# Attention and grouped feed-forward on one core: maximum pass with the norm folded in, group scalars spread by DMA, other places for the steps

## The chip, the cores and the metric

One Trainium2 chip, one core. The metric is device time in microseconds. The kernel before takes 446.42 us (median of 3 runs, 442.9 to 447.45).

## What is computed

x is (4, 256, 256): four sequences of 256 tokens with 256 channels. Two blocks are added to it in turn. In both, a two-way decayed scan (`wkv`) of a side input gives a gated input r, and the main part works on r. Cut to what matters:

```python
def qknorm(t, scale):
    return t * rsqrt(mean(t * t, -1) + 1e-6) * scale
# block 1: attention, 16 query heads on 4 key heads, head size 128, causal
q = qknorm((r @ Wq.T) by heads, q_scale); k = qknorm((r @ Wk.T) by heads, k_scale)
attn = softmax(where(causal, q @ k.T * 128 ** -0.5, min))
x = x + (attn @ v).reshape(b, t, 2048) @ Wo.T
# block 2: 64 experts in 8 groups, the best 8 of a token are kept
scores = softmax(r2 @ gate_w.T); w_e = scores kept only where in the top 8
flat = w_e[:, inv_map]              # (tokens, 8 groups, 8)
scalar = flat.sum(-1)               # one number for token and group
soft = softmax(where(flat == 0, -1e9, flat))
xg = r2 + soft @ mask_up_w          # (tokens, 8 groups, 256)
a = silu(xg @ gate_proj_w) * (xg @ up_proj_w)   # 176 rows for each group
x = x + sum over groups of scalar * (a @ down_proj_w)
```

## The kernel before

All activations lie transposed, channels on partitions. The weights of the matmuls that count are split into a high part (fp32r, ScalarE casts it) and a low part (GpSimd subtracts), and each product is three matmuls (`three`, L1103). Tokens go in two pairs of sequences (p = 0, 1) of 512 tokens.

Each engine runs a list of steps that `make_plan` (L115) writes once from a fixed order per engine (`ORDERS`, `FFN_ORDERS`), a starting list (`START`) and places for background steps (`bg`) and key and value steps (`kv`). An instruction waits only for semaphores; the order within an engine is that of its list.

- Start: the first `wkv` calls on VectorE and ScalarE, the key projections K1 and K3, and table steps R, which make a table of the experts' up projection (EX).
- Attention: 32 items m (a pair, a key head g, a sequence and a half t of it) run through a software pipeline of iterations i. An entry (kind, back) of an order treats item i - back in iteration i. A: projection of queries; ScalarE copies and squares; VectorE sums the squares (L902); N: norm of two items, ScalarE log and exp, VectorE one Newton step (`refine`, L908) to the inverse norms RQ. B: transposes of queries. C: scores on TensorE (L1176); then on VectorE (L1037) one pass per head that adds the mask to the scores, writes them to PR and gives the row maximum MX, and a small instruction (L1042) that makes the bias NBI = -MX * RQ. X: exp on ScalarE (L742, by way of L600) with scale RQ and bias NBI, which sums the row too. S: reciprocal on VectorE, multiplication on GpSimd (L587). D: transposes of the weights. E: product with V, copied to OH on ScalarE; L: OL on VectorE (L1063). F: projection with Wo. A unit u is 512 score columns: an even item has one unit of four heads with 128 keys, an odd one two units of two heads with 256 keys, 48 units in all.
- Feed-forward: 22 tiles f, 11 to a pair, of 128 of the 8 x 176 rows. GA and GB make gate and up in the banks sc and tr. GS (L1289) is one matmul of an indicator table IND with the split scalars SCX into the bank ov, and so spreads each row's group scalar over the partitions. GT: tanh on ScalarE. GU: three operations on VectorE (L1078, L1082, L1087), the third of which multiplies by ov. GH and GL split the result into OH and OL. Y(f) is TensorE's projection with the down weights, run two tiles later. Routing (`route`, L917, steps 0 to 8) makes the softmax, the top 8 and the scalars: for pair 0 in iterations 30 to 37, for pair 1 between the tiles. Step 8 transposes STS, in which the group sums stand twice, and VectorE makes the low part in rows 32 to 63 of SCX.
- The queue of SP issues every DMA, in order. Loads of weights go through three stage buffers in the order of TensorE's list (`load`, L472); each waits until the buffer's last user is done.

Of the kernel before, what the change touches and what calls it, by code (L numbers as in the profile page):

```python
# [26 lines left out]
NSTAGE, NSLOT, NPS = 3, 6, 4  # L27
# [5 lines left out]
def table_col(g):  # L33
# [24 lines left out]
    "PE": ["GA", "GB", "GS", "Y", "last", "split"],  # L58
# [18 lines left out]
def kv_k(p, half):  # L77
# [37 lines left out]
def make_plan(engine, order, ffn_order):  # L115
# [18 lines left out]
    for k, i in enumerate([25, 29]):  # L134
# [14 lines left out]
    for p, places in ((0, [3, 5, 6, 6]), (1, [20, 20, 23, 23])):  # L149
# [3 lines left out]
    for f, places in enumerate(([36, 37, 38], [45, 45, 45])):  # L153
        for kind, i in zip(("GA", "GB", "GS"), places):
# [38 lines left out]
    for st, f in zip(last, [0, 1, 2, 3, 4, 5, 6, 7, 8, 9, 10]):  # L193
# [25 lines left out]
BLOCKS = [s for s in PLAN if s[0] in ("small", "split", "ind") or s[0] == "R" and s[1] >= 6]  # L219
# [1141 lines left out]
```

## Time and profile before

| | us |
|---|---|
| median of 3 runs | 446.42 |
| lowest, highest | 442.9, 447.45 |
| the profiled execution, whole | 446.21 |
| its span, first to last instruction | 444.2 |

The span is what the profile accounts for; the other 2.0 us lie around it. Busy time is the time in which an engine has an instruction under way; overlapping instructions count once. "Idle before" is what passed on the engine before an instruction, with the one that released it. The stages follow one another: start up to about 44 us, attention up to about 331 us, then the feed-forward tiles.

### The profile page before, as it was taken

To read this page: it belongs to the slowest core of one execution; us is meant where nothing else is said; L and a number is where in the kernel's file an instruction comes from. 1 tells how busy PE (TensorE), PEld (TensorE's weight loads), DVE (VectorE), ACT (ScalarE), POOL (GpSimd) and SP (SyncE) were. 2 spreads that over 40 slices of the span, in tenths; PEclk is the share of its full clock that TensorE was granted. 3 is DMA by queue.
4 is the path that set the end of the run, shared out by engine and by line. 5 is a ranking of instruction groups with operands and counts; after the bars stand their busy time and mean duration, and the time that the engine had idled before them with its cause. 6 is when DMAs were issued, how large, how long until landed. Compare 5 with 4: busy or idle time off the path is not lost.

```text
span 444.2 us, 6572 instructions
## 1 busy us (share of the span) xinstructions
PE 380.3 (86%) x1974; PEld 305.6 (69%) x1974; DVE 336.3 (76%) x834; ACT 290.4 (65%) x675; POOL 214.8 (48%) x236
## 2 busy tenths in 40 slices
PE   0097866799998869997889798899899999999996
PEld 0086644587877557875758686777678887888884
DVE  6999577999998997577999979866657758553443
ACT  5444868699889768886789995979366334444321
POOL 4671520637553735513159121237138865687632
PEclk9998999999999997999999899999999999999999
DMA  7813410102111110110102200012112321233101
GB/s 201 312 32 106 137 43 0 49 1 97 47 49 48 49 47 0 49 49 0 47 2 82 80 0 2 0 38 71 38 53 90 106 53 56 72 108 94 61 0 47
DMA packets 11073, 26.84 MB, mean 60 GB/s; under 512 B 1312, under 2 KB 3872, under 8 KB 11040
## 3 DMA queue, kind: packets, MB, share of 16 engines
q1 hardware_dynamic: 11040, 26.44, 18.6%
q8 instruction: 16, 0.26, 0.2%
q14 instruction: 17, 0.14, 0.1%
HBM read 25.39 MB, written 1.05 MB: 60 GB/s over the span
## 4 chain that ended last, share of the span: by engine, by line
PE 49%; DVE 30%; ACT 12%; issue 6%; POOL 1%; DMA 1%; POOLq 0%; SPq 0%; DVEq 0%; ACTq 0%
PE acc L1105 4%; PE ov L1198 4%; PE acc L1106 4%; PE acc L1107 4%; PE tr L1127 4%; PE sc L1176 3%; DVE B L845 3%; DVE PR L1037 3%; DVE F L845 3%; ACT PR L600 3%; PE proj L1105 3%; PE proj L1107 2%; PE proj L1106 2%; DVE SS L902 2%; PE tr L1105 2%
## 5 line engine op out<-in xcount | busy, mean ns | idle before, releaser
L567 POOL TENSOR_TENSOR WL<-stage,WH 128x256 fp32r<-128x256 f32 x146 | 119.8, 851 | 112.7 <-ACT WH L637 112.6
L587 POOL TENSOR_TENSOR PR<-PR,RI 128x512 f32<-128x512 f32 x48 | 54.0, 1140 | 89.1 <-DVE RI L1051 89.1
L1105 PE MATMUL proj<-WH,RH 128*128 128x512 f32 x96 | 43.5, 453 | 39.3 <-DVE RL L896 22.9
L600 ACT ACTIVATE PR<-PR,NBI,RQ 128x128 f32<-128x128 f32 (+1 forms) x128 | 68.5, 546 | 1.9 <-DVE NBI L1042 1.7
L1105 PE MATMUL acc<-OH,WH 128*128 128x256 f32 (+1 forms) x172 | 55.4, 322 | 5.2 <-DVE OL L1063 4.4
L1107 PE MATMUL acc<-OH,WL 128*128 128x256 f32 (+1 forms) x172 | 54.0, 314 | 0.0
L1106 PE MATMUL acc<-OL,WH 128*128 128x256 f32 (+1 forms) x172 | 54.0, 314 | 0.0
L1176 PEld LDWEIGHTS sc<-kT,QT 128*128 128x128 f32 x256 | 40.8, 191 | 18.9 <-issue 14.1
L1105 PEld LDWEIGHTS proj<-WH,RH 128*128 128x128 f32 x96 | 19.0, 198 | 47.1 <-issue 42.5
L1176 PE MATMUL sc<-kT,QT 128*128 128x128 f32 (+1 forms) x256 | 47.5, 328 | 2.9 <-DVE MX L1037 2.9
L1198 PE MATMUL ov<-PTS,V 128*128 128x512 f32 x96 | 47.0, 598 | 1.4 <-DVE OL L1063 1.4
L637 ACT CAST WH<-stage 128x768 fp32r<-128x768 f32 (+1 forms) x42 | 39.4, 938 | 2.2 <-DMA stage<-in_wk 2.2
L1078 DVE SCALAR_TENSOR_TENSOR PR<-PR,sc 128x512 f32<-128x512 f32 x22 | 15.1, 685 | 32.2 <-ACT PR L792 32.2
L1107 PE MATMUL proj<-WH,RL 128*128 128x512 f32 x96 | 39.4, 410 | 0.0
L1106 PE MATMUL proj<-WL,RH 128*128 128x512 f32 x96 | 39.1, 408 | 0.0
L1037 DVE CUSTOM_DVE_ANT_0 PR<-sc,const 128x128 f32<-128x128 f32 (+1 forms) x128 | 39.0, 351 | 0.1
L1105 PEld LDWEIGHTS acc<-OH,WH 128*128 128x128 f32 x172 | 33.4, 194 | 7.9 <-issue 5.0
L593 POOL TENSOR_TENSOR OL<-PR,OH 128x512 fp32r<-128x512 f32 x22 | 28.7, 1307 | 12.6 <-ACT OH L800 12.6
L902 DVE TENSOR_REDUCE SS<-SQ 128x4 f32<-128x512 f32 x40 | 27.0, 677 | 10.3 <-ACT SQ L692 10.2
L1106 PEld LDWEIGHTS acc<-OL,WH 128*128 128x128 f32 x172 | 33.5, 195 | 1.7
L1107 PEld LDWEIGHTS acc<-OH,WL 128*128 128x128 f32 x172 | 33.4, 194 | 1.7
L800 ACT CAST OH<-PR 128x512 fp32r<-128x512 f32 x22 | 13.7, 622 | 30.3 <-PE acc L1107 28.4
(167 smaller groups left out, 913.1 us busy)
## 6 DMA issues: line engine op xcount, KB each, us to landing
stage<-in_ffn SPq DMA_DIRECT2D x22, 384.0 KB, 3.1
stage<-in_wq SPq DMA_DIRECT2D x8, 512.0 KB, 3.5
stage<-in_wo SPq DMA_DIRECT2D x8, 512.0 KB, 3.5
PR<-in_tables SPq DMA_DIRECT2D x4, 352.0 KB, 7.1
fT<-in_fT SPq DMA_DIRECT2D x4, 256.0 KB, 4.2
xT<-in_xT SPq DMA_DIRECT2D x4, 256.0 KB, 4.1
stage<-in_wk SPq DMA_DIRECT2D x2, 512.0 KB, 4.6
stage<-in_wv SPq DMA_DIRECT2D x2, 512.0 KB, 3.6
```

What stands on the lines that cost most here:

```text
L567: i = pool.tensor_tensor(lo[:, c:c + 256], src[:, c:c + 256], hi[:, c:c + 256].bitcast(F32), ALU.subtract)
L587: pool.tensor_tensor(pr, pr, RI[:, m % 4, hs[0]:hs[0] + nh].rearrange("p (h o) -> p h o", o=1).broadcast_to([P, nh, 512 // nh]), ALU.mult) ...
L593: pool.tensor_tensor(OL[:, sl], PR[:, 4 + f % 2, :], OH[:, sl].bitcast(F32), ALU.subtract).then_inc(s["a_lo"], 1)
L600: return nc.scalar.activation(o, i, ACT.Exp, **k)
L637: nc.scalar.copy(WH[:, slot, 0:w], src[:, 0:w]).then_inc(s["split_hi"], 1)
L902: v.tensor_reduce(SS[:, n % NST, half_, :], SQ[:, e % 2, :].rearrange("p (h n) -> p h n", h=REP), X, ALU.add).then_inc(s["sumsq_done"], 1)
L1037: i = v.tensor_tensor_reduce(PR[:, u % 6, w * k:w * k + w], sc[u % 2][:, w * k:w * k + w], mask[:, 256 - w:256], 1.0, NEG_BIG, ALU.add, AL ...
L1105: mm(o, lh, rh, start=first, stop=False, skip_group_check=True)
L1106: mm(o, lh, rl, start=False, stop=False, skip_group_check=True)
L1107: return mm(o, ll, rh, start=False, stop=last, skip_group_check=True)
L1176: i = mm(sc[u % 2][:, w * k:w * k + w], QT[:, m % 3, h, :], kT[:, g, T * bb:T * bb + w], start=True, stop=True)
L1198: i = mm(ov[:], V[:, 2 * bb + c, g * D:(g + 1) * D], PTS[:, m % 2, c, :, :].rearrange("p h n -> p (h n)"), start=(c == 0), stop=(c == ti))
```

## The change

Four things.

1. The maximum pass. The key scale `qks` and the Newton step change sign, so that RQ holds the negative inverse norm; the pass takes RQ as its factor, adds the mask, takes the minimum in place of the maximum and so writes scaled scores. MX is then the bias of exp itself, the exp's scale is the constant -1.0, and the bias instruction L1042 goes with its semaphore. The wait for RQ stands ahead of the pass.
2. The group scalars. IND, its two loads and two casts go, and the 22 GS matmuls. Route step 8 transposes the eight group sums alone, ScalarE copies them to SCR (8 partitions), and step 8 is gone from VectorE. SP spreads them: for each tile a DMA per group in it copies that group's row of 512 numbers from SCR to the partitions of that group in SBC (three buffers). The third operation of GU reads SBC in place of ov. On SP's queue the spread of tile f stands ahead of the load of tile f + 4, from f = 3 on it waits for GU(f - 3), and for route step 8 of its pair.
3. The orders. VectorE's C is at distance 1 at the end of the iteration, in place of distance 2 after the first key steps; F goes ahead of N and S. TensorE gets two more places for key and value steps; ScalarE's are in part moved behind X and N.
4. Places. In `START` TensorE runs the second K1 after one table step in place of three, ScalarE casts wk after the log and exp of the first scan and wq before its first K1, and VectorE sums the second squares earlier. Call (1, 1) of `wkv` comes an iteration or two earlier, and some splits, loads, V steps and routing steps move by one or two iterations.

```diff
-    "PE": [("kv", 0), ("kv", 0), ("kv", 0), ("kv", 0), ("D0", 4), ("bg", 0), ("A", 0),
-           ("kv", 0), ("D1", 4), ("kv", 0), ("F", 6), ("E", 5), ("bg", 0), ("C", 1),
-           ("B", 0), ("rest", 0)],
-    "ACT": [("kv", 0), ("kv", 0), ("kv", 0), ("kv", 0), ("kv", 0), ("D0", 4), ("kv", 0),
-            ("bg", 0), ("A", 0), ("X", 2), ("N", 0), ("E", 5), ("bg", 0), ("B", 0),
+    "PE": [("kv", 0), ("kv", 0), ("kv", 0), ("kv", 0), ("kv", 0), ("D0", 4), ("bg", 0),
+           ("A", 0), ("kv", 0), ("D1", 4), ("kv", 0), ("F", 6), ("E", 5), ("bg", 0),
+           ("kv", 0), ("C", 1), ("B", 0), ("rest", 0)],
+    "ACT": [("kv", 0), ("kv", 0), ("kv", 0), ("kv", 0), ("kv", 0), ("D0", 4), ("bg", 0),
+            ("A", 0), ("X", 2), ("N", 0), ("kv", 0), ("E", 5), ("bg", 0), ("B", 0),
             ("rest", 0)],
-    "DVE": [("kv", 0), ("kv", 0), ("kv", 0), ("kv", 0), ("C", 2), ("bg", 0), ("bg", 0),
-            ("A", 0), ("D1", 4), ("kv", 0), ("N", 0), ("S", 2), ("F", 6), ("rest", 0),
-            ("L", 5)],
+    "DVE": [("kv", 0), ("kv", 0), ("bg", 0), ("kv", 0), ("kv", 0), ("bg", 0), ("bg", 0),
+            ("A", 0), ("D1", 4), ("kv", 0), ("F", 6), ("N", 0), ("S", 2), ("rest", 0),
+            ("L", 5), ("C", 1)],
...
-    "PE": ["GA", "GB", "GS", "Y", "last", "split"],
+    "PE": ["GA", "GB", "Y", "last", "split"],
...
-    "PE": [("split", "K", 0), ("small",), ("split", "Q", 0), ("K1", 0, 0), ("R", 0), ("R", 1), ("R", 2),
-           ("K1", 0, 1), ("R", 3), ("R", 4), ("R", 5), ("K3", 0, 0), ("K3", 0, 1)],
+    "PE": [("split", "K", 0), ("small",), ("split", "Q", 0), ("K1", 0, 0), ("R", 0), ("K1", 0, 1), ("R", 1),
+           ("R", 2), ("R", 3), ("R", 4), ("R", 5), ("K3", 0, 0), ("K3", 0, 1)],
...
-    calls = {(1, 1): [1, 1, 1, 1, 1, 1, 1, 3, 3], (1, 2): [3, 4, 4, 5, 5, 6, 6, 7, 7], (1, 3): [7, 8, 8, 8, 10, 11, 12, 12, 12],
+    calls = {(1, 1): [0, 0, 0, 0, 0, 0, 0, 1, 1], (1, 2): [3, 4, 4, 5, 5, 6, 6, 7, 7], (1, 3): [7, 8, 8, 8, 10, 11, 12, 12, 12],
...
+def group_rows(m):
+
+    first, last = P * m // FI, (P * m + P - 1) // FI
+    return [(g, max(g * FI - P * m, 0), min((g + 1) * FI - P * m, P)) for g in range(first, last + 1)]
...
+            def spread_scalars(f):
+                p, m = divmod(f, FT)
+                sp.wait_ge(s["rt_act"], 7 * p + 7)
+                if f >= NBC:
+                    sp.wait_ge(s["a_ready"], f - NBC + 1)
+                for g, lo, hi in group_rows(m):
+                    sp.dma_start(SBC[lo:hi, f % NBC, :], SCR[g:g + 1, p * PT_:(p + 1) * PT_].rearrange("g (o n) -> g o n", o=1).broadcast_to([1, hi - lo, PT_])).then_inc(spread_in[f % NBC], 16)
+
             for n in range(6, len(BLOCKS)):
+                if BLOCKS[n][0:2] == ("split", "F") and BLOCKS[n][2] >= 4:
+                    spread_scalars(BLOCKS[n][2] - 4)
                 load(n)
+            for f in range(FT * NPAIR - 4, FT * NPAIR):
+                spread_scalars(f)
...
-                            i = exp(PR[:, u % 6, w * k:w * k + w], PR[:, u % 6, w * k:w * k + w], bias=NBI[:, m % 4, h:h + 1],
-                                    scale=RQ[:, n % NST, half_, h:h + 1], accum_out=RS[:, m % 4, h:h + 1])
+                            i = exp(PR[:, u % 6, w * k:w * k + w], PR[:, u % 6, w * k:w * k + w], bias=MX[:, m % 4, h:h + 1],
+                                    scale=-1.0, accum_out=RS[:, m % 4, h:h + 1])
...
-                        nc.scalar.copy(SCX[:, tok], proj[:]).then_inc(s["rt_act"], 1)
+                        nc.scalar.copy(SCR[:, tok], proj[0:G, :]).then_inc(s["rt_act"], 1)
...
-            v.tensor_scalar(qks[:], vecs[:, 8:9], vecs[:, 9:10], float(D) ** -0.5, ALU.mult, ALU.mult).then_inc(s["key_scale_ready"], 1)
+            v.tensor_scalar(qks[:], vecs[:, 8:9], vecs[:, 9:10], -float(D) ** -0.5, ALU.mult, ALU.mult).then_inc(s["key_scale_ready"], 1)
...
+                    dve.wait_ge(s["rq_ready"], n + 1)
                     for j in range(ti + 1):
...
-                            i = v.tensor_tensor_reduce(PR[:, u % 6, w * k:w * k + w], sc[u % 2][:, w * k:w * k + w],
-                                                       mask[:, 256 - w:256], 1.0, NEG_BIG, ALU.add, ALU.max, MX[:, m % 4, h:h + 1])
+                            i = v.tensor_tensor_reduce(PR[:, u % 6, w * k:w * k + w], sc[u % 2][:, w * k:w * k + w], mask[:, 256 - w:256],
+                                                       RQ[:, n % NST, half_, h:h + 1], BIG, ALU.add, ALU.min, MX[:, m % 4, h:h + 1])
                         i.then_inc(s["max_ready"], 1)
-                        dve.wait_ge(s["max_ready"], u + 1)
-                        dve.wait_ge(s["rq_ready"], n + 1)
-                        v.scalar_tensor_tensor(out=NBI[:, m % 4, hs[0]:hs[0] + nh], in0=MX[:, m % 4, hs[0]:hs[0] + nh], scalar=-1.0,
-                                               in1=RQ[:, n % NST, half_, hs[0]:hs[0] + nh], op0=ALU.mult, op1=ALU.mult).then_inc(s["bias_ready"], 1)
...
-                    dve.wait_ge(s["scal_full"], f + 1)
+                    dve.wait_ge(spread_in[f % NBC], 16 * spread_count(f))
...
-                    v.scalar_tensor_tensor(out=PR[:, 4 + f % 2, :], in0=PR[:, 2 + f % 2, :], scalar=0.5, in1=ov[:],
+                    v.scalar_tensor_tensor(out=PR[:, 4 + f % 2, :], in0=PR[:, 2 + f % 2, :], scalar=0.5, in1=SBC[:, f % NBC, :],
                                            op0=ALU.mult, op1=ALU.mult).then_inc(s["a_ready"], 1)
...
-                    mm(ov[:], IND[:, P * m:P * m + P], SCX[:, p * PT_:(p + 1) * PT_], start=True, stop=True).then_inc(s["scal_full"], 1)
```

## Rows read from the trace of the kernel before

**Rows 1.** The page, busy time, share of the span, instructions
```profile
PE 380.3 (86%) x1974; PEld 305.6 (69%) x1974; DVE 336.3 (76%) x834; ACT 290.4 (65%) x675; POOL 214.8 (48%) x236
```
**Rows 2.** The page, chain that ended last, share of the span by engine
```profile
PE 49%; DVE 30%; ACT 12%; issue 6%; POOL 1%; DMA 1%; POOLq 0%; SPq 0%; DVEq 0%; ACTq 0%
```
**Rows 3.** Windows: stretch, length, busy by engine, clock, DMA share, GB/s
```profile
10.00:20.00 10.00, 0.00 (x0) 0.00 (x0) 9.79 (x13) 4.20 (x6) 7.91 (x9) 1.00 0.98 352
44.00:331.00 287.00, 252.78 (x1404) 199.74 (x1404) 234.11 (x671) 225.37 (x565) 122.70 (x131) 0.98 0.13 41
331.00:438.00 107.00, 106.79 (x483) 87.70 (x482) 62.92 (x107) 44.59 (x71) 69.49 (x79) 1.00 0.23 69
```
**Rows 4.** Waits of TensorE: us in total, times, longest
```profile
PE proj L1105 <- DVE RL L896: 22.9, 1, 22.9
...
PE proj L1105 <- ACT SQ L692: 7.1, 6, 1.5
...
PE acc L1105 <- DVE OL L1063: 4.4, 3, 2.2
```
**Rows 5.** Timeline of the last tiles: start, length, instruction, idle before
```profile
430.00 0.69 DVE L1078 SCALAR_TENSOR_TENSOR PR<-PR,sc 128x512 f32<-128x512 f32 x1 [2.34 <-ACT PR L792]
...
434.76 0.69 DVE L1078 SCALAR_TENSOR_TENSOR PR<-PR,sc 128x512 f32<-128x512 f32 x1 [2.33 <-ACT PR L792]
...
435.51 0.39 PE L1289 MATMUL ov<-SCX,IND 128*128 128x512 f32 x1
...
435.74 0.39 PE L1105 MATMUL acc<-OH,WH 128*128 128x512 f32 x1
...
439.38 0.50 PE L1105 MATMUL acc<-OH,WH 128*128 128x512 f32 x1 [0.76 <-POOL OL L593]
```
**Rows 6.** Groups by line, the GS matmul: busy us, mean ns, idle before
```profile
L1289 PE MATMUL ov<-SCX,IND 128*128 128x512 f32 x22 | 8.6, 389 | 0.0
```
**Rows 7.** DMA issues: count, size, median us from issue to landing
```profile
stage<-in_ffn SPq DMA_DIRECT2D x22, 384.0 KB, 3.1
...
out<-xT SPq DMA_DIRECT2D x4, 256.0 KB, 2.8
```
**Rows 8.** Single lines: ns at least, median, at most; first and last start
```profile
L877 DVE TENSOR_TENSOR F<-F,B x8: 679/685/1216, 16.2 to 275.2; 128x512 f32<-128x512 f32 x8
...
L567 POOL TENSOR_TENSOR WL<-stage,WH x146: 714/742/1727, 13.7 to 422.7; 128x256 fp32r<-128x256 f32 x146
```
**Rows 9.** Groups by line on VectorE, as in rows 6
```profile
L1042 DVE SCALAR_TENSOR_TENSOR NBI<-MX,RQ 128x2 f32<-128x2 f32 (+1 forms) x48 | 17.3, 360 | 1.7
...
L889 DVE SCALAR_TENSOR_TENSOR F<-E 128x512 f32<-128x512 f32 x8 | 5.5, 693 | 0.3
...
L892 DVE SCALAR_TENSOR_TENSOR F<-F,half_mix 128x512 f32<-128x512 f32 x4 | 3.0, 753 | 0.1
```
**Rows 10.** Groups by line on ScalarE, shapes apart, as in rows 6
```profile
L600 ACT ACTIVATE PR<-PR,NBI,RQ 128x256 f32<-128x256 f32 x64 | 37.7, 601 | 1.9 <-DVE NBI L1042 1.7
...
L600 ACT ACTIVATE EUX<-fT,vecs 128x256 f32<-128x256 f32 x16 | 7.2, 499 | 0.0
...
L600 ACT ACTIVATE RT<-RT 128x256 f32<-128x256 f32 x4 | 1.7, 418 | 1.7 <-DVE RT L962 1.7
```
**Rows 11.** Timeline of the start on TensorE, ScalarE and GpSimd
```profile
12.27 1.05 ACT L637 CAST WH<-stage 128x1024 fp32r<-128x1024 f32 x1 [2.19 <-DMA stage<-in_wk]
...
13.74 4.21 POOL L567 TENSOR_TENSOR WL<-stage,WH 128x256 fp32r<-128x256 f32 x4
...
28.13 1.04 ACT L637 CAST WH<-stage 128x1024 fp32r<-128x1024 f32 x1
...
30.81 0.52 PE L1105 MATMUL proj<-WH,RH 128*128 128x512 f32 x1
...
38.71 1.70 PE L1127 MATMUL tr<-const,RT 128*128 128x128 f32 x8 [2.65 <-DVE RT L1003]
```
**Rows 12.** Timeline at route step 8 of pair 0, ScalarE
```profile
327.53 0.59 ACT L784 CAST SCX<-proj 128x512 fp32r<-128x512 f32 x1 [1.07 <-PE proj L1246]
```

More of the change, by code:

```diff
@@ L26 @@
 NEG_BIG = -1.0e30
-NSTAGE, NSLOT, NPS = 3, 6, 4
+BIG = 3.0e38
+NSTAGE, NSLOT, NPS, NBC = 3, 6, 4, 3
 KCAP = 30.0
@@ L94 @@
 RELEVANT = {
-    "PE": {"R": None, "split": None, "small": None, "ind": None, "K1": None, "V": None, "K3": None, "GA": None, "GB": None,
-           "GS": None, "route": (0, 1, 3, 4, 6, 7, 8)},
-    "ACT": {"split": None, "small": None, "ind": None, "K1": None, "V": None, "K2": None, "K3": None, "table": None,
+    "PE": {"R": None, "split": None, "small": None, "K1": None, "V": None, "K3": None, "GA": None, "GB": None,
+           "route": (0, 1, 3, 4, 6, 7, 8)},
+    "ACT": {"split": None, "small": None, "K1": None, "V": None, "K2": None, "K3": None, "table": None,
             "wkv": (1, 6, 7), "gate": (0, 1), "route": (0, 2, 3, 5, 6, 7, 8)},
     "DVE": {"K1": None, "K2": None, "table": None, "onehot": None, "wkv": (0, 2, 3, 4, 5, 6, 8), "gate": (0, 1),
-            "route": (1, 2, 4, 5, 6, 7, 8)},
+            "route": (1, 2, 4, 5, 6, 7)},
     "POOL": {"split": None, "small": None, "zeros": None},
@@ L133, in make_plan @@
             put(bg, i, st)
-    for k, i in enumerate([25, 29]):
+    for k, i in enumerate([27, 29]):
         put(bg, i, ("gate", 0, k))
@@ L137, in make_plan @@
         put(bg, i, ("route", 0, k))
-    for n, back in enumerate([-2, -2, -2, -1, -4, -2, -2, -3]):
+    for n, back in enumerate([-2, -2, -2, -1, -3, -2, -2, -3]):
         put(bg, max(first_tile(*divmod(n, NKV)) + back, 0), ("split", "Q", n))
-    for n, on in enumerate([5, 5, 5, 5, 4, 5, 5, 5]):
+    for n, on in enumerate([5, 5, 5, 5, 5, 5, 5, 4]):
         put(bg, first_tile(*divmod(n, NKV)) + on, ("split", "O", n))
-    early = [32, 36, 38]
+    early = [33, 37, 39]
     for f, i in enumerate(early):
@@ L148, in make_plan @@
             put(kv, i, st)
-    for p, places in ((0, [3, 5, 6, 6]), (1, [20, 20, 23, 23])):
+    for p, places in ((0, [3, 5, 6, 6]), (1, [21, 21, 24, 24])):
         for t, i in enumerate(places):
@@ L152, in make_plan @@
     ahead = []
-    for f, places in enumerate(([36, 37, 38], [45, 45, 45])):
-        for kind, i in zip(("GA", "GB", "GS"), places):
+    for f, places in enumerate(([36, 37, 37], [45, 45, 45])):
+        for kind, i in zip(("GA", "GB"), places):
             if i < END:
@@ L192, in make_plan @@
     per = {f: [] for f in range(NF)}
-    for st, f in zip(last, [0, 1, 2, 3, 4, 5, 6, 7, 8, 9, 10]):
+    for st, f in zip(last, [0, 1, 2, 3, 4, 5, 6, 6, 8, 9, 10]):
         if concerns(engine, st):
@@ L217 @@
 PLAN = PLANS["PE"]
-BLOCKS = [s for s in PLAN if s[0] in ("small", "split", "ind") or s[0] == "R" and s[1] >= 6]
+BLOCKS = [s for s in PLAN if s[0] in ("small", "split") or s[0] == "R" and s[1] >= 6]
 BLOCK_NO = {s: n for n, s in enumerate(BLOCKS)}
@@ L306, with spread_count @@
         unit_tr[units_before(_m) + _j] = TR[("D", _m, _j)]
+def group_rows(m):
+    first, last = P * m // FI, (P * m + P - 1) // FI
+    return [(g, max(g * FI - P * m, 0), min((g + 1) * FI - P * m, P)) for g in range(first, last + 1)]
+def spread_count(f):
+    return sum(len(group_rows(k % FT)) for k in range(f % NBC, f + 1, NBC))
 def program(nc, ins, out):
@@ L421, in program @@
         staged = [sem(f"staged{k}") for k in range(NSTAGE)]
+        spread_in = [sem(f"spread_in{k}") for k in range(NBC)]
         block = ctx.enter_context(nc.Block())
@@ L721, in _ @@
                     i.then_inc(s["table_hi"], 1)
-                elif st[0] == "ind":
-                    w, blk = FT * P // 2, BLOCK_NO[st]
-                    act.wait_ge(staged[blk % NSTAGE], 16 * (blk // NSTAGE + 1))
-                    nc.scalar.copy(IND[:, w * st[1]:w * st[1] + w], stage[:, blk % NSTAGE, 0:w]).then_inc(s["indicator_ready"], 1)
                 elif st[0] == "B":
```

83 lines of the change are left out of this document (29 added, 54 removed).

## Prediction

> **What bounds the kernel now.** I read the page's busy shares first, then its chain of waits. TensorE is busy 86% of the span and VectorE 76% [rows 1], but the chain that ended last stands on TensorE for 49%, on VectorE for 30% and on ScalarE for 12% [rows 2]: more than one engine sets the pace. The windows say where [rows 3]. From 331 to 438 us, the stage of the 22 feed-forward tiles, TensorE is busy for 106.79 of 107 us, so that stage is TensorE's alone. Before it, from 44 to 331 us, TensorE is busy 252.78 of 287 us, VectorE 234.11 and ScalarE 225.37. No engine is full there and no wait of TensorE is long: the largest totals behind its start are 7.1 us for ScalarE's square and 4.4 for the low halves of O on VectorE [rows 4]. TensorE's busy time overstates that stage too, as matmuls overlap (a 128x512 matmul is booked at 389 ns and the next starts 0.23 us later, [rows 5, 6]). It is a net of hand-overs between engines that run in fixed order. Ahead of all that TensorE waits 22.9 us for the first decayed rows [rows 4].
>
> **The matmul that goes (GS).** One matmul per tile, 22 of them, in a stage where TensorE never pauses. The busy sum is 8.6 us [rows 6], but the next matmul starts 0.23 us after it (435.51 to 435.74), and a tile, which comes every 4.76 us (430.00 to 434.76, [rows 5]), holds 21 of them (6 + 1 for gate, 6 + 1 for up, GS, 6 for Y): 0.227 us a slot. The last one isn't on the path: after it the chain is GU, OH, OL, then Y, for which TensorE already waits 0.76 us [rows 5]. So 21 x 0.227 = **4.8 us saved**. Its steps of preparation go too: two casts on ScalarE and two loads, in the attention stage, where they weigh little.
>
> **What replaces it: the spread by DMA.** Per tile 256 KB, one row of SBUF copied to 128 partitions (36 DMAs for 22 tiles, as 14 tiles touch two groups). They go on SP's queue, ahead of the load of tile f+4. A spread may start once GU(f-3) is done and is needed by the third operation of GU(f), three tiles or some 13 us later, so its latency is hidden; if that cover goes, each excess us delays every tile. Behind it on SP waits the load of tile f+4, which is wanted three tiles later: hidden. At the change of pair, spread 11 waits for route step 8 in tile 10, and the third GU of tile 11 is wanted some 4.6 us later (14 slots and two operations of 0.69); the copy of 0.6 us and a DMA of 3 us fit, and if not, Y comes two tiles later and hides an us. Throughput is what remains. No row shows a DMA from one partition. The nearest rows are the store of 256 KB in 2.8 us, from 128 partitions [rows 7], and the peak of 352 GB/s over 16 engines at 98% busy, 22 GB/s each [rows 3]. Were one source row served like one engine's stream, a spread would take 262,144 B / 22 GB/s = 11.9 us. A tile then lasts 4.53 us, and its own load of 393,216 B takes 1.1 us at the peak rate. So the spread is free up to about 3.4 us and sets the pace above. I take 2.8 to 3.4, cost nothing, because 128 packets of 2 KB spread over 16 engines are what the store also is, and carry the other end as a rival.
>
> The trace shows no transfer whose source is one partition. The Trainium skill, "SBUF — State Buffer", section "Door 1: The DMA port swizzle", speaks against this edit: four neighbouring partitions share one port, and one port gave 27.6 GB/s. By that rule a spread would take 262,144 / 27.6 GB/s = 9.5 us, an estimate from that page, and the 22 tiles would be paced at 10.6 us, for a total near 560 us. No run here shows it.
>
> The third GU now reads two SBUF operands. Such an operation on VectorE (L877) took 679 to 1,216 ns, and a quarter of a split on GpSimd 714 to 1,727 [rows 8]. If all 22 meet, VectorE loses 22 x 0.53 = 12 us and GpSimd as much; but in this stage VectorE is busy 62.92 and GpSimd 69.49 of 107 us [rows 3], so both hide it. At the tail GpSimd has no split left, so nothing there.
>
> **The maximum pass.** 48 bias steps go, 17.3 us busy at 360 ns plus 1.7 us idle before them [rows 9]: 19.0 us of VectorE. In return the 128 passes take their scale from a tile. A scalar-tensor-tensor over 128x512 took 693 ns with an immediate and 753 with such an operand [rows 9]: 0.06 us, so 0 to 7.7 us; I take half, 3.8, as the pass is another instruction. Two small writes and a subtraction of routing go in either pair; I leave them out of the sum. Net **15 us** of VectorE. The pass now waits for the inverse norm before it starts; that is computed by the same engine three steps earlier in the iteration, so no new wait; if it were late, L and the next iteration's steps would queue behind it.
>
> ScalarE gains as well: exp now has an immediate scale. Exps over 128x256 took 418 ns with no tile operand (RT), 499 with one (EUX) and 601 with two (PR) [rows 10]. The last of these sums its row too, so the scale is worth 0 to 0.10 us; the step before it, 0.08, points to most of it. 128 x 0.10 = **13 us** of ScalarE, 0 at the least. The rows can't part the operand from the sum. The Trainium skill, "ScalarE: Activation LUTs", section "What ACT_TABLE_LOAD costs", gives about 93 ns for each such operand; by it, an estimate from that page, the gain is 11.9 us.
>
> How much of this reaches the end? Outside the feed-forward stage the chain stands on VectorE for 0.30 x 444.2 = 133 us, of 336.3 - 62.9 = 273 us busy: 49%. ScalarE: 53 of 290.4 - 44.6 = 246 us, 22% [rows 1, 2, 3]. First order, 15 x 0.49 + 13 x 0.22 = 7.4 + 2.9 = **10.3 us**. At the least it is what ScalarE waited for the bias, 1.7 us [rows 10]. At the most all 19 us, for VectorE is the fuller of the two slower engines there.
>
> **The order.** Written round the loop, VectorE's iteration is nearly the old one: C at distance 1 at the end is C at distance 2 at the start, with the steps for keys between them moved behind. TensorE's and ScalarE's lists only move the key and value steps. So I cost the iterations at nothing, with +-4 us for reordering. The start can be followed. TensorE did three table steps before the second K1 at 30.81 [rows 11]; now it does one, and the second K1 waits for ScalarE, which now casts wq (1.04 us) before the first K1's copy and square, not after, and squares until about 29.2. So K1 ends near 30.7 instead of 32.5. The key norm then isn't queued behind VectorE's four steps on the denominators but before them, and its 0.5 us wait for ScalarE is covered. The first key transpose, at 38.71 after 2.65 us of idle time [rows 11], moves to about 38.0: **0.7 us saved**. ScalarE's cast of wk slides from 12.27 to about 17.6, behind the log and exp of the first call; with its 1.05 us and GpSimd's 4.21 us [rows 11] the split ends near 22.8, where TensorE starts at 22.9: level, 0.2 us lost if not. Route steps and splits move by an iteration at most.
>
> **Sum against the profiled execution.** Span 444.2, its run 446.2, 2.0 around it, and 446.4 is the median of three. 446.2 - 4.8 - 10.3 - 0.7 = 430.4; I forecast **430 us**, 0.964 of before.
>
> **Rivals.**
> 1. Full relief: attention is VectorE's, all 19 us arrive, plus 4.8 and some of ScalarE's: 446.2 - 4.8 - 19 - 3 = 419 us. For it: VectorE is 82% busy there, the most of the three if TensorE's overlap is taken out. Against it: half of the chain there is not on VectorE.
> 2. The relief is absorbed: each engine's list is fixed, and the next hand-over (TensorE's O projection, ScalarE's square) ends the wait. Then 4.8 + 1.7 + 0.7 = 7.2, giving 439 us. For it: waits are many and short [rows 4].
> 3. The new places and the waits they bring take back what the rest gives, 446 us. The 4 us of the order's range, with the relief absorbed as in rival 2, come to 443; it takes 3 us more, from moved routing and F steps that I can't follow. Against it: the order round the loop hardly changes.
> 4. Slower: the one source row limits the spread. It decides from 3.4 us per spread. At 11.9 us, tiles come every 11.9 + 1.1 = 13.0 us, from route step 8's end (copy from 327.53 for 0.59 us [rows 12], less 11 gained) on: 317 + 22 x 13.0 + 8 of tail + 2 = 613 us. For it: all 16 engines ask one row, and no row of the trace shows that to be quick. Against it: the row is only 2 KB and packets of the same size and number take 2.8 us when stored.
>
> **Chances.** Forecast (424 to 435): 0.42. Full relief (below 424): 0.15. Absorbed (435 to 441.5): 0.18. Cancelled (441.5 to 451): 0.08. Spread bound (above): 0.17. What a measurement of this kernel can tell from no change is about 1%, or 4.5 us. Faster by more than that: 0.42 + 0.15 + 0.18 = 0.75; within it 0.08; slower 0.17. The range from 416 to 445 leaves out the spread-bound case and about 0.03 at either end together, 0.2 in all.
>
> **What would show it.** In the profile after: a GU third operation every 4.53 us between 4 and 11 us sooner; TensorE full in the feed-forward stage; DMA issues of SBC landing in about 3 us, with no wait of L1087's successor for them (a wait of DVE for a DMA of SBC there is rival 4, and its length is the price). The 128-wide and 256-wide exp near 390 and 500 ns shows ScalarE's term; the max pass at 284 to 344 and 417 to 477 ns shows VectorE's. First O tile done some 11 us earlier in the stage before 331 us shows the share that arrives; if it is 2, rival 2; if TensorE's idle time goes up while VectorE's busy falls, rival 3. I'm wrong if the spread lands after 3.4 us, or if the exp does not shorten and the passes lengthen by the full 0.06.

## The result and the profile after

| | us |
|---|---|
| before, median of 4 runs | 445.08 |
| after, median of 4 runs | 535.51 (534.2 to 537.24) |
| ratio after / before | 1.2033, 95% interval 1.1953 to 1.2113 |
| span of the profiled execution, before and after | 444.2 and 533.3 |

The changed kernel is 20% slower, where 430 us was forecast. Rival 4 happened: the spread of the scalars from one row of SBUF sets the pace of the last stage.

The page of the kernel after: busy time, then three rows of the 40 slices, DMA share, and the chain of work that ended last. It answers [rows 1] and [rows 2].

```profile
PE 393.2 (74%) x1952; PEld 308.0 (58%) x1952; DVE 326.5 (61%) x780; ACT 275.4 (52%) x673; POOL 216.2 (41%) x235
...
PE   0388678999989989799889995674965908757533
...
PEclk9999999999999999989999997796977977897956
DMA  7623101210112100220001139998989999999883
...
PE 28%; DVE 20%; SPq 18%; DMA 15%; ACT 11%; issue 7%; POOL 2%; POOLq 0%; DVEq 0%; ACTq 0%
DMA SBC<-SCR 14%; SPq L544 12%; SPq L503 5%; PE ov L1205 5%; PE sc L1183 4%; PE tr L1134 4%; PE proj L1112 3%; DVE B L860 3%; PE acc L1112 2%; DVE F L860 2%; PE acc L1114 2%; PE acc L1113 2%; PE proj L1114 2%; PE proj L1113 2%; DVE PR L1048 2%
```

Read the slices first. Through the first 24 slices (320 us) the kernel looks as before, and from there TensorE falls from nine tenths to about six while the DMA row goes to nine. The chain, which stood on TensorE for 49% [rows 2], now stands on SP's issues and on DMAs for 33% together, and its first line is the spread.

The windows of the kernel after: us, busy time (instructions) of TensorE, its loads, VectorE, ScalarE, GpSimd, then TensorE's granted clock, DMA share, GB/s.

```profile
44.00:317.00 273.00, 243.81 (x1390) 193.06 (x1389) 225.36 (x618) 208.80 (x560) 122.88 (x128) 0.99 0.12 37
317.00:524.00 207.00, 127.36 (x462) 96.27 (x460) 60.47 (x102) 43.38 (x71) 70.09 (x82) 0.81 0.91 64
```

The feed-forward stage was 107 us with TensorE full [rows 3]; it is 207 us with TensorE at 127. The last two numbers of its row give the kind of limit away: the DMA engines are busy for 91% and move 64 GB/s, where 98% busy meant 352 GB/s in [rows 3]. A high share with few bytes means that the engines wait and don't transfer; e5 below moves as many packets and bytes in half the busy time. TensorE was granted 0.81, a mean between its two levels of 1.2 and 2.4 GHz, in a stage with sixteen pauses of 2.3 to 14.1 us; before, it paused here for 0.2 us in all and had its full clock.

The waits of the kernel after, VectorE and TensorE: us in total, times, longest.

```profile
DVE PR L1094 <- DMA SBC<-SCR: 126.4, 21, 7.0
...
PE acc L1112 <- POOL OL L613: 48.2, 12, 6.7
...
PE acc L1112 <- DVE xT L1103: 14.1, 1, 14.1
```

VectorE's timeline in the same stage: start, duration, what ended the idle time before.

```profile
477.04 0.69 DVE L1094 SCALAR_TENSOR_TENSOR PR<-PR,SBC 128x512 f32<-128x512 f32 x1 [4.66 <-DMA SBC<-SCR]
478.92 0.69 DVE L1085 SCALAR_TENSOR_TENSOR PR<-PR,sc 128x512 f32<-128x512 f32 x1 [1.18 <-ACT PR L807]
479.71 0.69 DVE L1089 TENSOR_TENSOR PR<-PR,tr 128x512 f32<-128x512 f32 x1
486.75 0.69 DVE L1094 SCALAR_TENSOR_TENSOR PR<-PR,SBC 128x512 f32<-128x512 f32 x1 [6.35 <-DMA SBC<-SCR]
...
496.36 0.69 DVE L1094 SCALAR_TENSOR_TENSOR PR<-PR,SBC 128x512 f32<-128x512 f32 x1 [6.26 <-DMA SBC<-SCR]
```

The third GU (L1094) comes every 9.7 us (477.04, 486.75, 496.36), and before 21 of the 22 VectorE waits for the spread, 126.4 us in all. TensorE's waits for OL are the same wait one step later. 262,144 B in 9.7 us are 27.0 GB/s.

The DMA issues of the kernel after: KB each, median us from issue to landing.

```profile
stage<-in_ffn SPq DMA_DIRECT2D x22, 384.0 KB, 13.9
...
SBC<-SCR SPq DMA_DIRECT2D x8, 256.0 KB, 15.2
...
SBC<-SCR SPq DMA_DIRECT2D x4, 32.0 KB, 13.8
```

A spread of 32 KB lands as late as one of 256 KB: the landing time is the queue ahead, not the transfer. The weight loads, from HBM and to all partitions, went from 3.1 us [rows 7] to 13.9 because they stand in the same queue (in e5 below, with the same queue and another source, they take 3.3).

Where the 89.1 us between the spans are: up to the first third GU, which came at 333.18 before and comes at 325.97 now, 7.2 gained; from it to the last one 103.3 before and 198.2 now, 94.9 lost; behind it 7.7 before and 9.1 now, 1.4 lost.

The attention stage did gain. Its end, ScalarE's copy of route step 8:

```profile
313.45 0.58 ACT L799 COPY SCR<-proj 8x512 f32<-8x512 f32 x1 [1.80 <-PE proj L1253]
```

It was at 327.53 [rows 12]: 14.1 us sooner. This is one trace of each; in the eight traces below of kernels with parts 1, 3 and 4 the copy comes at 311.1 to 318.1 us. Half of the gain is gone by the first third GU, which waited 7.04 us for the first spread. The groups by shape, VectorE's pass and then ScalarE's exp (busy us, mean ns | idle before). Before, as far as [rows 10] doesn't show them:

```profile
L1037 DVE CUSTOM_DVE_ANT_0 PR<-sc,const 128x256 f32<-128x256 f32 x64 | 24.3, 417 | 0.0
L1037 DVE CUSTOM_DVE_ANT_0 PR<-sc,const 128x128 f32<-128x128 f32 x64 | 14.6, 284 | 0.0
L600 ACT ACTIVATE PR<-PR,NBI,RQ 128x128 f32<-128x128 f32 x64 | 30.8, 491 | 0.0
```

After:

```profile
L1048 DVE CUSTOM_DVE_ANT_0 PR<-sc,const,RQ 128x256 f32<-128x256 f32 x64 | 27.0, 477 | 0.0
L1048 DVE CUSTOM_DVE_ANT_0 PR<-sc,const,RQ 128x128 f32<-128x128 f32 x64 | 18.5, 344 | 0.0
```
```profile
L620 ACT ACTIVATE PR<-PR,MX 128x256 f32<-128x256 f32 x64 | 31.7, 510 | 0.2 <-DVE MX L1048 0.2
L620 ACT ACTIVATE PR<-PR,MX 128x128 f32<-128x128 f32 x64 | 24.9, 402 | 0.2 <-DVE MX L1048 0.2
```

The scaled pass takes 60 ns more than the plain one, the full upper bound of the prediction; exp takes 91 ns less (601 in [rows 10]) and 89 less at 128 wide.

### The profile page after: what moved, and what is told of

Same layout as the page of the kernel before. It is cut to its first block, busy times and chain, and to the rows that moved or that the text cites. A ratio compares the mean times of both kernels' runs of the same rounds, so it can differ in the third digit from the quotient of the medians.

```text
span 533.3 us, 6457 instructions
## 1 busy us (share of the span) xinstructions
PE 393.2 (74%) x1952; PEld 308.0 (58%) x1952; DVE 326.5 (61%) x780; ACT 275.4 (52%) x673; POOL 216.2 (41%) x235
## 4 chain that ended last, share of the span: by engine, by line
PE 28%; DVE 20%; SPq 18%; DMA 15%; ACT 11%; issue 7%; POOL 2%; POOLq 0%; DVEq 0%; ACTq 0%
DMA SBC<-SCR 14%; SPq L544 12%; SPq L503 5%; PE ov L1205 5%; PE sc L1183 4%; PE tr L1134 4%; PE proj L1112 3%; DVE B L860 3%; PE acc L1112 2%; DVE F L860 2%; PE acc L1114 2%; PE acc L1113 2%; PE proj L1114 2%; PE proj L1113 2%; DVE PR L1048 2%
## 5 line engine op out<-in xcount | busy, mean ns | idle before, releaser
L1112 PE MATMUL acc<-OH,WH 128*128 128x256 f32 (+1 forms) x172 | 59.8, 348 | 63.4 <-POOL OL L613 48.2
L1094 DVE SCALAR_TENSOR_TENSOR PR<-PR,SBC 128x512 f32<-128x512 f32 x22 | 15.6, 708 | 126.5 <-DMA SBC<-SCR 126.4
L607 POOL TENSOR_TENSOR PR<-PR,RI 128x512 f32<-128x512 f32 x48 | 55.2, 1164 | 90.8 <-DVE RI L1058 90.8
L1114 PE MATMUL acc<-OH,WL 128*128 128x256 f32 (+1 forms) x172 | 57.4, 333 | 0.0
L1113 PE MATMUL acc<-OL,WH 128*128 128x256 f32 (+1 forms) x172 | 57.0, 331 | 0.0
L620 ACT ACTIVATE PR<-PR,MX 128x128 f32<-128x128 f32 (+1 forms) x128 | 56.6, 456 | 0.3 <-DVE MX L1048 0.3
L1048 DVE CUSTOM_DVE_ANT_0 PR<-sc,const,RQ 128x128 f32<-128x128 f32 (+1 forms) x128 | 45.5, 411 | 0.1
L1114 PEld LDWEIGHTS acc<-OH,WL 128*128 128x128 f32 x172 | 34.7, 202 | 2.8
L1113 PEld LDWEIGHTS acc<-OL,WH 128*128 128x128 f32 x172 | 34.6, 201 | 1.8
## 6 DMA issues: line engine op xcount, KB each, us to landing
stage<-in_ffn SPq DMA_DIRECT2D x22, 384.0 KB, 13.9
SBC<-SCR SPq DMA_DIRECT2D x8, 256.0 KB, 15.2
```

Of the source, the lines that this page charges most:

```text
L607: pool.tensor_tensor(pr, pr, RI[:, m % 4, hs[0]:hs[0] + nh].rearrange("p (h o) -> p h o", o=1).broadcast_to([P, nh, 512 // nh]), ALU.mult) ...
L620: return nc.scalar.activation(o, i, ACT.Exp, **k)
L1048: i = v.tensor_tensor_reduce(PR[:, u % 6, w * k:w * k + w], sc[u % 2][:, w * k:w * k + w], mask[:, 256 - w:256], RQ[:, n % NST, half_, h:h ...
L1112: mm(o, lh, rh, start=first, stop=False, skip_group_check=True)
L1113: mm(o, lh, rl, start=False, stop=False, skip_group_check=True)
L1114: return mm(o, ll, rh, start=False, stop=last, skip_group_check=True)
```

## The experiments

Three questions: which part costs the time, what about the spread costs it, and what the other parts are worth. The kernel before, measured beside them, had medians of 444.59 us (e1 to e4), 444.92 (e5 to e8) and 443.23 (e9 to e12); each ratio is against the kernel before as measured beside it.

### Which part: e1 to e4

**e1_gs_back**: the changed kernel with part 2 undone.

```diff
-                    v.scalar_tensor_tensor(..., in1=SBC[:, f % NBC, :], ...)
+                    v.scalar_tensor_tensor(..., in1=ov[:], ...)
+                    mm(ov[:], IND[:, P * m:P * m + P], SCX[:, p * PT_:(p + 1) * PT_], ...)
```

> The changed kernel with part 2 undone: GS matmuls, their table and split scalars are back, the pass, orders and places stay. If the spread is the whole of the loss, the feed-forward tiles come every 4.76 us again and the gain of the attention stage (route step 8's copy on ScalarE at 313.45 us after against 327.53 before, 14.1 us) is what remains: 445 - 14 = 431 us. If the new orders or the pass also cost something in the feed-forward stage, it stays above 436.

Measured: 439.94 us (438.3 to 443.03), ratio 0.9913 (0.9877 to 0.9949). The tile period is 4.86 us, not 4.76, and one tile has a new wait, both below; so the second of the two cases, with 9 us more than the 431 of the first.

**e4_spread_only**: the kernel before with part 2 alone (IND, SCX and GS out, SCR, SBC and the 36 DMAs in).

> The kernel before with the spread by DMA alone. If one source row limits the spread, tiles come every 9.7 us as in the changed kernel and the loss is that of 22 tiles: route step 8's copy stays near 327.5, so 327.5 + 22 x 9.7 + 8 = 549 us, some 14 above the changed kernel. If the loss needed the new places too (late loads, late splits), it is well below 530.

Measured: 551.81 us, ratio 1.244 (1.2373 to 1.2507). VectorE waits for the spread 131.8 us in 22 waits; the tile period is 9.8 us.

So the spread alone makes the slowdown, whatever stands around it: undone, the kernel is 0.9% faster than before, and alone it costs 24%.

**e2_max_only**: the kernel before with part 1 alone.

```diff
-    v.tensor_tensor_reduce(..., mask[:, 256 - w:256], 1.0, NEG_BIG, ALU.add, ALU.max, MX[...])
+    v.tensor_tensor_reduce(..., mask[:, 256 - w:256], RQ[...], BIG, ALU.add, ALU.min, MX[...])
```

> The kernel before with the scaled maximum pass alone. If the lighter engines bring the attention stage's 14 us, about 433 us (at least 9 of the 14 us). If the new places bring them, 441 to 446. By the first-order sum of the prediction with the sizes that the changed kernel showed (VectorE 19.0 - 7.7, at 49%, ScalarE 128 x 0.091 at 22%): 5.5 + 2.6 = 8.1 us, 437.

Measured: 441.36 us, ratio 0.9951 (0.991 to 0.9993).

**e3_order_only**: the kernel before with the orders and places alone (parts 3 and 4).

> The kernel before with the new orders, start and places alone (bias steps and GS stay). If the places are worth what the pass leaves of the 14 us, about 6 us: 439. If they only pay once the pass is lighter, 445 or slower. If they alone bring the stage's gain, 432.

Measured: 446.91 us, ratio 1.0061 (1.0025 to 1.0097). Alone, the orders and places cost 0.6%.

e2 lies at the lower end of the case "the new places bring them" (441 to 446) and 4 us above its sum; e3 is slower than before, which leaves the places alone with no gain at all. Both fell short of the sum, and the traces showed two things that were in no sum: a tile period of 4.86 us instead of 4.76, and in e1 and e3 one new wait of TensorE. The wait of e1 (us in total, times, longest); in e3 it is 2.2 us:

```profile
PE ov L1286 <- DVE PR L1084: 2.1, 1, 2.1
```

One of the moved routing steps of pair 1 (step 5, from tile 7 to tile 6) puts VectorE's routing operations between two GUs, and the next GS waits for the bank that the late GU still reads. e10 and e11 below take both up.

### What about the spread: e5 to e8 and e12

**e5_wide_source**: the same DMAs to the same places, but each reads as many partitions as it writes.

```diff
-    sp.dma_start(SBC[lo:hi, f % NBC, :], SCR[g:g + 1, ...].rearrange(...).broadcast_to([1, hi - lo, PT_]))
+    sp.dma_start(SBC[lo:hi, f % NBC, :], E2[lo:hi, 0:PT_])
```

> The changed kernel, with the spread's 36 DMAs unchanged in number, size, queue and destination, but reading 128 partitions of a scan buffer (E2) in place of one row each: the group scalars are left out, so the output is another. If the single source row is the limit, a spread lands in about 3 us, VectorE does not wait for it and tiles come every 4.5 us: about 427 us. If any SBUF to SBUF copy of this size is slow, or the queue with 36 more issues is, tiles stay near 9.7 us and the time at 535.

Measured: 429.01 us (427.66 and 430.36), ratio 0.9655 (0.9583 to 0.9727). The DMA issues of e5:

```profile
stage<-in_ffn SPq DMA_DIRECT2D x22, 384.0 KB, 3.3
SBC<-E SPq DMA_DIRECT2D x8, 256.0 KB, 3.2
```

The DMA queue (packets, MB, share of 16 engines) of the changed kernel and of e5:

```profile
q1 hardware_dynamic: 14144, 31.49, 46.0%
```
```profile
q1 hardware_dynamic: 14144, 31.49, 23.3%
```

As many DMAs, as many packets, as many bytes, and 106 us less. The limit is on the reading side; the queue, the issue and the write are the same in both.

**e6_half_row**: 1 KB of each row in place of 2 KB, in as many packets; the third GU uses the half twice.

```diff
-    sp.dma_start(SBC[lo:hi, f % NBC, :], SCR[g:g + 1, p * PT_:(p + 1) * PT_]...)
+    sp.dma_start(SBC[lo:hi, f % NBC, 0:PT_ // 2], SCR[g:g + 1, p * PT_:p * PT_ + PT_ // 2]...)
```

> The changed kernel with half the bytes in each packet: each spread copies 256 of the 512 numbers (1 KB to each of 128 partitions, as many packets as before), and the third operation reads them twice, so half the tokens get other tokens' scalars. If bytes from one row are the limit (27 GB/s), a spread takes 4.85 us and tiles come every 4.9 to 5.2 us: about 435 us. If the number of packets is the limit, they stay at 9.7 us and 535.

Measured: 435.81 us, ratio 0.9808 (0.9743 to 0.9873). VectorE waits 20.7 us for the spread, and in the second pair the third GU comes every 4.83 to 4.93 us in tiles 12 to 15. That is half of 9.7 (4.85): the time goes with the bytes, none of it with the packets, and the tile's own load, which is whole in both, adds nothing that shows.

**e7_two_ports**: the eight rows stand twice, in partitions g and 64 + g, and each spread is cut in two DMAs that read one copy each.

```diff
+        parts += [(g, lo, mid), (64 + g, mid, hi)]
...
+    linked(v.tensor_copy(SG8[:, :, 64:64 + G], g8a[:]))
```

> The changed kernel with each group's row standing twice, in partition g and in partition 64 + g, and each DMA halved: one half of the destination reads the first, the other half the second. If the limit is one row's way out and two rows have ways of their own that work side by side, tiles come every 4.9 to 5.5 us, about 437 us. If all 16 engines go through the halves one after the other, or the limit is not the source row, tiles stay at 9.7 us and 535.

Measured: 460.23 us, ratio 1.0358 (1.0259 to 1.0456): most of the loss is gone, though not as much as the first case expected.

**e12_same_port**: e7 with the second copy in partition 32 + g.

```diff
-        parts += [(g, lo, mid), (64 + g, mid, hi)]
+        parts += [(g, lo, mid), (32 + g, mid, hi)]
```

> As e7 (the rows at two partitions, each half of a spread from its own), but the second copy lies at partition 32+g, not 64+g. If what limits is the one partition, two partitions give what e7 gave: 5.9 us per tile and about 460 us. If it is a port that both partitions share, nothing is gained over one: 9.7 us per tile and about 535 us.

Measured: 537.82 us (537.06 and 538.58), ratio 1.2144 (1.2057 to 1.2231). VectorE's wait for the spread (us in total, times, longest), first e7, then e12:

```profile
DVE PR L1106 <- DMA SBC<-SCR: 42.4, 19, 4.7
```
```profile
DVE PR L1106 <- DMA SBC<-SCR: 125.7, 21, 7.0
```

The DMA issues of the largest halves (KB each, median us to landing), e7 and e12:

```profile
SBC<-SCR SPq DMA_DIRECT2D x20, 128.0 KB, 7.1
```
```profile
SBC<-SCR SPq DMA_DIRECT2D x20, 128.0 KB, 11.4
```

The two kernels differ only in where the copy lies. With it 64 partitions away a tile takes 5.9 us on the average ((447.67 - 323.52) / 21); 32 away, 9.4 us ((527.58 - 329.24) / 21) with 9.6 to 9.7 as the steady value, as with one row. So the limit isn't the partition but something that partitions g and 32 + g share and 64 + g doesn't, at 27.0 GB/s. The Trainium skill, "SBUF — State Buffer", section "Door 1: The DMA port swizzle", names it: 32 partitions further is the same port and 64 further another, and one port gave 27.6 GB/s. These runs agree, with 27.0. Why two ports gave 5.9 us and not 4.85 was not tried; the halves of a spread stand one behind the other in the one queue, which lets one port idle in turn, but that is only argued. (For comparison, e8 below, which almost no spread holds up, averages 4.82: (421.99 - 320.80) / 21.)

The changed kernel has a smaller sign of the same. Tiles 5 and 16 are those whose two DMAs read partitions 3 and 4; their third GU follows the one before after 9.03 and 8.01 us (9.17 and 7.60 in e4), where tiles that read other neighbouring pairs take 9.6 to 9.9. This was not followed further.

**e8_hbm_bounce**: the eight rows are stored once per pair to HBM, and the spreads read them there, still one row to many partitions.

```diff
+    if m == 0:
+        sp.dma_start(scal[:, tok], SCR[:, tok]).then_inc(bounced, 16)
+        sp.wait_ge(bounced, 16 * (p + 1))
...
-    sp.dma_start(SBC[lo:hi, f % NBC, :], SCR[g:g + 1, ...]...)
+    sp.dma_start(SBC[lo:hi, f % NBC, :], scal[g:g + 1, ...]...)
```

> The changed kernel with the eight rows (16 KB) stored to HBM once for each pair, and the spreads read from there, one row of HBM to 128 partitions. If only the source row in SBUF was slow, tiles come every 4.5 us and what the prediction wanted of the change is there: 431 - 4.8 = 427 us (the two extra round trips of some 2.5 us are hidden or cost 1 us each). If many engines reading one row are slow wherever it lies, tiles stay above 6 us and the time above 470.

Measured: 431.0 us (429.35 to 431.78), ratio 0.9687 (0.9634 to 0.9741); nothing of the computation is left out. It is 13.9 us faster than the kernel before and 104.5 faster than the changed one. The DMA issues of e8, and then the group of its third GU (busy us, mean ns | idle before):

```profile
stage<-in_ffn SPq DMA_DIRECT2D x22, 384.0 KB, 3.3
SBC<-scal_bounce SPq DMA_DIRECT2D x8, 256.0 KB, 3.9
```
```profile
L1098 DVE SCALAR_TENSOR_TENSOR PR<-PR,SBC 128x512 f32<-128x512 f32 x22 | 22.2, 1011 | 4.0 <-DMA SBC<-scal_bounce 2.1
```

One row read 128 times is no trouble in HBM: 3.9 us where it was 15.2, with the queue ahead in the latter. Two microseconds of wait are left, once, at the first tile of the second pair, where the store and the spread follow route step 8:

```profile
377.24 0.82 DVE L1098 SCALAR_TENSOR_TENSOR PR<-PR,SBC 128x512 f32<-128x512 f32 x1 [2.05 <-DMA SBC<-scal_bounce]
```

### The other parts, again: e9 to e11

In the last stage the kernels fell into two families. With the 64-byte tile NBI still allocated (before, e3) a tile takes 4.76 us; without it (e1, e2) 4.86, and 4.63 in e5 and e8, which have no GS. The removal of NBI moves every SBUF tile allocated behind it by 64 bytes.

**e9_hbm_pad**: e8 with NBI allocated and never used.

```diff
-        MX, RS, RI = (sb(n, [P, 4, REP]) for n in ("MX", "RS", "RI"))
+        MX, NBI, RS, RI = (sb(n, [P, 4, REP]) for n in ("MX", "NBI", "RS", "RI"))
```

> The kernel of e8 (spread from HBM) with the 64-byte tile NBI of the kernel before kept in its place and never used, so that every SBUF tile allocated after it lies at the address it had before. Nothing else differs. Theory 'addresses': in the stage of the last tiles the kernels that keep the tile take 0.2267 us per matmul slot and those without it 0.2315 us. If the shift of 64 bytes is the cause, the tile period goes from 4.63 to 4.53 us, 21 x 0.10 = 2.1 us, and the time from 431.0 to about 428.5. Rival 'the lighter mix of work': the slot has to do with what the engines do beside it; then the period stays 4.63 and the time 431.

Measured: 430.09 us (426.95 to 432.83), ratio 0.9709 (0.9632 to 0.9787). The tile period is 4.53, as expected, but the whole can't be told from e8. TensorE's groups from 350 to 420 us, e8 and then e9:

```profile
L1118 PE MATMUL acc<-OH,WL 128*128 128x512 f32 x28 | 11.1, 395 | 0.0
L1117 PE MATMUL acc<-OL,WH 128*128 128x512 f32 x28 | 11.1, 395 | 0.0
L1116 PE MATMUL acc<-OH,WH 128*128 128x512 f32 x28 | 11.0, 394 | 0.0
```
```profile
L1116 PE MATMUL acc<-OH,WH 128*128 128x512 f32 x30 | 11.8, 392 | 0.0
...
L1118 PE MATMUL acc<-OH,WL 128*128 128x512 f32 x30 | 11.7, 390 | 0.0
L1117 PE MATMUL acc<-OL,WH 128*128 128x512 f32 x30 | 11.7, 390 | 0.0
```

**e10_max_pad**: e2 with the same line.

> The kernel of e2 (scaled maximum pass alone) with the 64-byte tile NBI kept and unused. Addresses: the tile period goes from 4.86 to 4.76 us, the time from 441.4 to about 439, which is then the whole of what the scaled maximum pass is worth by itself (about 6 us). Rival: period 4.86 and 441.4 as in e2.

Measured: 437.03 us (434.6 to 441.18), ratio 0.9866 (0.9832 to 0.99), against 0.9951 (0.991 to 0.9993) for e2. The tile period is 4.76. One unused 64-byte tile is worth 0.8% here. 21 tiles of 0.09 give 1.8 us of it (105.1 to 103.3 between the first and the last third GU). The rest would lie ahead of the tiles, and that isn't shown: route step 8's copy comes 3.7 us sooner in e10 than in e2 (317.49 and 321.21), but 1.8 us later in e9 than in e8 (317.05 and 315.21).

**e11_gs_pad_place**: e1 with the unused tile and with route step 5 in the tile of before.

```diff
-    for st, f in zip(last, [0, 1, 2, 3, 4, 5, 6, 6, 8, 9, 10]):
+    for st, f in zip(last, [0, 1, 2, 3, 4, 5, 6, 7, 8, 9, 10]):
```

> The kernel of e1 (the change with the GS matmul back) with the 64-byte tile kept and step 5 of the routing in the tiles of before, the one step whose new place showed a PE wait of 2.1 us. Expected: 439.9 - 2.1 (addresses) - 2.1 (wait) = about 436. Against e9 at 428.5 this would leave 7 us for the GS matmul where the sum had 4.8; if the wait was hidden in something else, 438 and 9 us.

Measured: 436.17 us (435.19 to 436.74), ratio 0.9842 (0.9787 to 0.9898). It is what was expected. The wait of 2.1 us is gone, and the distances of the third GUs are those of the kernel before, 103.3 us over all.

## Why the prediction was wrong, step by step

**The stage is TensorE's alone.** Right for the kernel before, and for e8 and e9, where TensorE is busy 103.4 and 103.7 of 105 us.

**The spread costed at nothing.** This is the step that failed. Its reasoning was that "128 packets of 2 KB spread over 16 engines are what the store also is". Packets were the wrong thing to compare: e6 has as many packets and half the time, e5 as many packets from many partitions and 3.2 us. What counts is how many ports the bytes come from (e7 and e12), and the store of [rows 7] read 128 partitions. So where 2.8 to 3.4 us stood, a spread takes 9.7, and every tile with it. The threshold of 3.4 us, 4.53 less 1.1 for the tile's load, was too low as well, since the load adds nothing (e6); no run has a spread between the 3.9 us of e8 from issue to landing, which is free, and the 4.85 of e6, which paces the tiles.

**Its latency is hidden, and the load behind it too.** In e5 both were: VectorE waits for no spread there. In the changed kernel neither was: once the spread is the bound, everything behind it is late by the same amount (loads 3.1 to 13.9 us). The three buffers only shift this by three tiles.

**Rival 4** had the mechanism, the place and the sign. Its size was too high: 613 us against 535.5. Two terms were off. The rate of one source row was read as 22 GB/s from the mean over 16 engines, and it is 27.0. And the tile's load of 1.1 us was added, while e6 shows that it adds nothing (4.85 us for half the bytes, 9.7 for all). With 9.7 us a tile the same sum is 317 + 22 x 9.7 + 8 + 2 = 540. The port figure of 27.6 GB/s from the Trainium skill, "SBUF — State Buffer", section "Door 1: The DMA port swizzle", which the prediction worked out in a sentence apart, gives 9.5 us a spread as an estimate; 9.7 was measured. The chance of 0.17 was too low for a case in which no row spoke for the forecast but an analogy.

**GS, 4.8 us.** The slot was right: the steady tile goes from 4.76 (e11) to 4.53 us (e9). Of 21 x 0.23, the traces show 2.9 us between the first and the last gate projection (107.1 to 104.2), as TensorE now waits elsewhere in the first ten tiles; 1.0 us of these waits can be named (0.2 for OL, 0.6 of issue, 0.2 for SX), the rest was not followed. The pair isn't GS alone either: e9 has route step 5 in tile 6 and e11 in tile 7, though e9 shows no wait of 2.1 us for it. The medians give 6.1 us (436.17 and 430.09), with intervals that take in both. The prediction had the sign and about the size.

**Third GU with two SBUF operands.** Right. In e8 it takes 1,011 ns on the average, 0.32 more than before (689) and within the 0.53 us allowed, and VectorE hides it. It takes 0.69 us wherever GpSimd has no instruction under way beside it, in e8 as in the changed kernel, and up to 1.62 where it has one.

**Maximum pass.** VectorE's net gain is 19.0 - 128 x 0.060 = 11.3 us, not 15. ScalarE's is 128 x 0.090 = 11.5, not 13; the Trainium skill, "ScalarE: Activation LUTs", section "What ACT_TABLE_LOAD costs", has about 93 ns for such an operand, and 89 and 91 are measured. By the factors of the prediction, 11.3 x 0.49 + 11.5 x 0.22 = 8.1 us. e10 gives 443.23 - 437.03 = 6.2 us: between absorbed and forecast. So the weights by the chain were a fair guide in this one case, a little high.

**Orders, start and places.** Costed at 0 within 4 us, and 0.7 for the start. e11 against e10, both in the addresses of before and without the wait of 2.1 us, is 436.17 against 437.03, and the ratios overlap. Nothing can be measured. The 0.7 us at the key transpose can't be told: in the ten traces with the new start the first one comes at 35.65 to 39.43 us, in the four with the old start at 37.04 to 38.71. TensorE's first matmul, which the prediction held level at 22.9, did come sooner, at 21.8 to 22.3 against 22.5 to 22.9. What was missed is the one wait that a moved routing step brought: its 2.2 us are nearly all of the 2.3 that e3 loses.

**The addresses.** No step of the prediction had them, since NBI's removal was booked as a saving alone. It took back about half of what the lighter pass brings: 3.2 us are left in e2, 6.2 in e10.

**The sum.** With the reading side widened (e5) the kernel takes 429.0 us, from HBM (e8) 431.0, and 430 was forecast. That this fits so closely is partly luck: the maximum pass gave less than its 10.3 us, the step from e11 to e9 6.1 us by the medians where 4.8 stood. Some scatter of the spans goes with TensorE's granted clock (two runs of e9: 431.0 us at 0.983 and 425.9 at 0.996, the first with its full clock in the last stage), so single traces were used here for periods and waits, and medians for totals.

## What to carry to other kernels

Before a DMA replaces an engine's work, ask how many partitions each side of it touches and how they lie, not only how many bytes or packets it has: a broadcast from one row of SBUF is paced by the port of that row, and a copy of the row 32 partitions away is behind the same one. A DMA share near one with few GB/s in the windows is its signature; keep the source in HBM (e8), or leave the broadcast to a matmul, as before; a second copy of the row 64 partitions away helped, but not enough (e7). And when a buffer goes, keep its bytes allocated in one variant: what the removed work was worth and what moved addresses cost can be measured apart.

## What the runs showed of the hardware

- One row of SBUF read by 16 DMA engines gives 27.0 GB/s (262,144 B in 9.7 us); a second copy 32 partitions away adds nothing (9.6 to 9.7 us), one 64 away brings the tile to 5.9 us, and 256 KB from a row in HBM land in 3.9 us.
- While the DMAs ahead are held up, SP's own issues take longer. Min, median and max ns of the issues of the spreads and of the tiles' loads, in the changed kernel and then in e5:

```profile
L544 SPq DMA_DIRECT2D SBC<-SCR x36: 517/2346/8944, 314.1 to 502.1; - x36
L503 SPq DMA_DIRECT2D stage<-in_ffn x22: 327/790/7697, 232.2 to 474.2; - x22
```
```profile
L545 SPq DMA_DIRECT2D SBC<-E x36: 475/535/1122, 311.7 to 405.1; - x36
L503 SPq DMA_DIRECT2D stage<-in_ffn x22: 327/333/591, 230.1 to 391.3; - x22
```

- With the tiles allocated behind NBI moved by 64 bytes, the 128x512 matmuls of Y take 395 ns in place of 390 to 392 in the records, and TensorE's steady slot is 4.63 / 20 = 0.2315 us in place of 4.53 / 20 = 0.2265. Two pairs of kernels that differ in one unused 64-byte tile show it (e8 and e9, e2 and e10). Which tile's address matters was not tried. It isn't only that of a matmul's own operands: by the distances between starts in e8 and e9, some 0.04 us of the 0.10 fall on the six matmuls of a tile that read OH and OL, which move, and about as much on the twelve that read WH, RH and RL, which stand ahead of NBI.
- A scale from a tile in place of an immediate costs VectorE's masked pass 60 ns, whether 128 or 256 wide (the pass takes the minimum in place of the maximum besides); an immediate in place of a tile saves ScalarE's exp 89 to 91 ns.
